# Cross-attention with split 16-bit products: result copies before the exp, context maxima two tiles earlier, a shorter context scale, the first low part transposed later

## The reference

```python
q = (x @ Wq + bq); k = (ctx @ Wk + bk); v = (ctx @ Wv + bv)     # 16 heads of 64
attn = softmax(q k^T / 8)                                         # per head, over 1444 keys
out  = (attn v) @ Wo + bo
z    = x + out
y    = (z - mean(z)) / sqrt(var(z) + 1e-5) * gamma + beta
```

## Time and profile before

| | |
|---|---|
| median of the runs | 945.15 us |
| the profiled execution, its own time | 943.91 us |
| its span in the profile | 942.0 us |
| busy PE / DVE / ACT / POOL | 892.3 / 830.2 / 754.6 / 281.9 us |
| granted PE clock, mean over the span | 0.989 of 2.4 GHz |

### The profile page before, as it was taken

How to read it: one execution, slowest core, us unless ns; L and a number is a source line. 1 busy time by engine, 2 the same in 40 slices (tenths; PEclk the granted TensorE clock), 3 DMA queues, 4 the chain that set the end, 5 groups by cost and what they waited for, 6 DMA issues and landing times.

```text
span 942.0 us, 25453 instructions
## 1 busy us (share of the span) xinstructions
PE 892.3 (95%) x10366; PEld 673.4 (71%) x10366; DVE 830.2 (88%) x1072; ACT 754.6 (80%) x1082; POOL 281.9 (30%) x368
## 2 busy tenths in 40 slices
PE   7797998999999999999999999999999999999996
PEld 6475876777777776777777777777777676677775
DVE  4897889999898999989799998989999798998983
ACT  3675978888888888888888878888888888888983
POOL 3051394413214141232404223141412424042001
PEclk9998999999999999999999999999999999999999
DMA  8676999999999999999999999999999999999995
GB/s 224 133 159 143 186 175 163 204 203 187 220 181 205 201 214 205 201 213 183 208 198 206 211 178 211 193 215 201 197 212 192 198 196 196 198 183 203 204 178 112
DMA packets 683065, 181.17 MB, mean 192 GB/s; under 512 B 654596, under 2 KB 682052, under 8 KB 682948
## 3 DMA queue, kind: packets, MB, share of 16 engines
q1 hardware_dynamic: 681332, 178.48, 99.3%
q10 hardware_dynamic: 1344, 0.53, 0.2%
q0 software_dynamic: 272, 0.53, 0.2%
HBM read 15.35 MB, written 0.82 MB: 17 GB/s over the span
## 4 chain that ended last, share of the span: by engine, by line
PE 51%; DVE 22%; issue 8%; DMA 8%; POOL 5%; ACT 4%; SPq 1%; POOLq 0%; DVEq 0%; ACTq 0%
PE ps L530 21%; PE ps L544 15%; DVE p_lo L765 9%; PE ps L549 8%; DVE nmax L750 8%; DMA pt_lo<-p_lo 7%; PE ps L399 4%; PE ps L393 2%; DVE c_max L670 1%; ACT p L868 1%; POOL c_lo L975 1%; POOL early_sb L1003 1%; ACT c_hi L850 1%; POOL c_scaled L1001 1%; ACT o_t L891 1%
## 5 line engine op out<-in xcount | busy, mean ns | idle before, releaser
L765 DVE SCALAR_TENSOR_TENSOR p_lo<-p,rinv,p_hi 128x1444 f16<-128x1444 f32 x200 | 352.3, 1762 | 19.5 <-DMA pt_lo<-p_lo 17.2
L868 ACT ACTIVATE p<-ps,nmax 128x1446 f32<-128x1446 f32 x200 | 292.2, 1461 | 89.8 <-DVE nmax L750 89.1
L750 DVE TENSOR_REDUCE nmax<-ps 128x1 f32<-128x1446 f32 x200 | 331.5, 1658 | 36.3 <-PE ps L530 32.6
L876 ACT ACTIVATE p_hi<-p,rinv 128x1444 f16<-128x1444 f32 x200 | 299.8, 1499 | 39.0 <-DVE rinv L758 37.5
L544 PE MATMUL ps<-pt_hi,c_hi 128*128 128x128 f16 (+1 forms) x2288 | 270.0, 217 | 27.9 <-ACT o_t L891 25.2
L544 PEld LDWEIGHTS ps<-pt_hi,c_hi 128*128 128x128 f16 x2288 | 216.0, 98 | 76.2 <-ACT o_t L891 64.1
L544 PE MATMUL ps<-pt_hi,c_lo 128*128 128x128 f16 (+1 forms) x2288 | 269.3, 217 | 0.0
L544 PEld LDWEIGHTS ps<-pt_hi,c_lo 128*128 128x128 f16 x2288 | 217.5, 98 | 12.0 <-issue 0.2
L530 PE MATMUL ps<-ct_hi,g_hi 128*128 128x482 f16 (+3 forms) x624 | 157.2, 370 | 2.1 <-DMA ct_hi<-c_hi 2.1
L549 PE MATMUL ps<-pt_lo,c_hi 128*128 128x128 f16 (+1 forms) x2288 | 157.5, 217 | 0.0
L530 PE MATMUL ps<-ct_hi,g_lo 128*128 128x482 f16 (+3 forms) x624 | 157.1, 370 | 0.0
(11 more groups left out here) (108 smaller groups left out, 654.0 us busy)
## 6 DMA issues: line engine op xcount, KB each, us to landing
c_raw<-in_ctx_dram SPq DMA_DIRECT2D x32, 256.0 KB
pt_hi<-p_hi SPq DMA_TRANSPOSE x200, 3.5
pt_lo<-p_lo SPq DMA_TRANSPOSE x200, 3.7
c_raw<-in_ctx_dram SPq DMA_DIRECT2D x16, 192.0 KB
c_raw<-in_ctx_dram SPq DMA_DIRECT2D x48, 18.0 KB
out_dram<-y SPq DMA_DIRECT2D x16, 50.0 KB
x_sb<-in_x_dram SPq DMA_DIRECT2D x1, 600.0 KB
o_t<-in_L_xattn_Wq_dram SPq DMA_DIRECT2D x2, 256.0 KB, 4.4
```

Source lines behind the costliest of these rows:

```text
L750: dve.tensor_reduce(nmax[:, n % RING:n % RING + 1], ps[:, bank:bank + 3, 0:KEYW], AX.XY, ALU.max, negate=True).then_inc(s_nm, 1)
L765: dve.scalar_tensor_tensor(out=p_lo[:, par, 0:KL], in0=p32[:, n % P32S, 0:KL], scalar=rinv[:, i:i + 1], in1=p_hi[:, par, 0:KL], op0=ALU.mu ...
L868: act.activation(p32[:, n % P32S, :].rearrange("p (k w) -> p k w", w=KEYW), ps[:, bank:bank + 3, 0:KEYW], ACT.Exp, bias=nmax[:, i:i + 1], ...
L876: act.activation(p_hi[:, par, 0:KL], p32[:, n % P32S, 0:KL], ACT.Copy, scale=rinv[:, i:i + 1]).then_inc(s_hi, 1)
```

## The change

- ACT: `take_result(n-4)` stands before `exponentials(n)` instead of behind it, in every tile.
- The thirds of the context's high part are at r = 4, 6, 7 instead of 4, 5, 6.
- The context maxima are at r = 6, 7, 8 instead of 8, 9, 10; the spreading matmul and `context_scale` at r = 10 instead of 11, except in window 0.
- `context_scale` is two DVE instructions instead of three: a constant column of 1e-30 joins the maxima, and the identity by which the matmul spreads them is scaled by 1/32 beforehand (`ident_part`), so that the reduction writes `unscale` directly.
- The subtraction and scaling of the layer norm (`norm_rows`) go from DVE to POOL, into `scale_rows`; z, zn, zg and y live in the space of `wo_sb`, now called `late_sb`.
- SP: `ct_hi` at r = 7, `ct_lo` at r = 8, and in window 0 at r = 9.

```diff
-    CMAX_AT = 8
+    CMAX_AT = 6
-    CT_LO_AT = 7
+    CT_LO_AT = 8
+    CT_LO_AT_FIRST = 9
...
-                dve.tensor_reduce(c_top[:, :], bank[:, 0:P], AX.X, ALU.max).then_inc(s_ctop, 1)
-                dve.wait_ge(s_ctop, b + 1)
...
-                dve.tensor_scalar(un, c_top[:, :], C_LEAST, 1.0 / C_RANGE, ALU.max, ALU.mult).then_inc(s_us, 1)
+                dve.tensor_reduce(un, bank[:, 0:P], AX.X, ALU.max).then_inc(s_us, 1)
...
-                if r == TOP_AT and w > 0:
-                    norm_rows(w - 1)
...
             for n in range(N + LAG):
+                if n >= LAG:
+                    take_result(n - LAG)
                 if n < N:
                     exponentials(n)
-                if n >= LAG:
-                    take_result(n - LAG)
...
+            pool.tensor_scalar(ident_part[:, :], ident[:, :], 1.0 / C_RANGE, 1.0, ALU.mult, ALU.mult).then_inc(s_part_id, 1)
...
             def scale_rows(b):
                 par = b % 2
+                pool.wait_ge(s_rd, b + 1)
+                pool.tensor_scalar(zn[:, par, :], z[:, par, :], mv[:, par, 0:1], rstd[:, par:par + 1], ALU.subtract,
+                                   ALU.mult).then_inc(s_zn, 1)
```

More of the change, by code:

```diff
@@ L58, in cross_attention_kernel @@
     STORE_AT = 2
-    CHI_AT = 4
+    CHI_AT = (4, 6, 7)
     FIN_AT = 6
-    CMAX_AT = 8
-    CT_HI_AT = 6
-    CT_LO_AT = 7
+    CMAX_AT = 6
+    CT_HI_AT = 7
+    CT_LO_AT = 8
+    CT_LO_AT_FIRST = 9
     ROWS_AT = 9
-    TOP_AT = 11
+    TOP_AT = 10
+    TOP_AT_FIRST = 11
     def first_tile(b):
@@ L111, in cross_attention_kernel @@
         ident = sb("ident", [P, P])
+        ident_part = sb("ident_part", [P, P])
         early_sb = sb("early_sb", [P, 4, PAIRS, P])
@@ L118, in cross_attention_kernel @@
             "p (b i q) -> p b i q", i=2, q=QL)
-        wo_sb = sb("wo_sb", [P, PAIRS, P])
+        late_sb = sb("late_sb", [P, PAIRS, P])
+        wo_sb = late_sb
+        z, zn, zg, y = [late_sb[0:QL, 2 * i:2 * i + 2, :] for i in range(4)]
         bv_sb = sb("bv_sb", [P, PAIRS])
@@ L177, in cross_attention_kernel @@
         s_axt = sem("ax_max_spread")
-        s_ctop = sem("context_max_on_every_partition")
+        s_part_id = sem("identity_over_range_ready")
         s_const = sem("constants_set")
@@ L193, in cross_attention_kernel @@
         s_axz = sem("ax_parts_zeroed")
+        s_cleast = sem("least_context_max_set")
         s_ax = sem("ax_group_max")
@@ L358, in _ @@
                     transpose_context_hi(w + 1)
-                if r == CT_LO_AT and w + 1 < B:
+                if r == (CT_LO_AT if w else CT_LO_AT_FIRST) and w + 1 < B:
                     transpose_context_lo(w + 1)
@@ L450, in spread_context_max @@
                 pe.wait_ge(s_cm, b + 1)
-                pe.matmul(bank[:, 0:P], spread(c_max[:, NT:NT + 1]), ident[:, :], start=True, stop=True).then_inc(s_top, 1)
+                pe.wait_ge(s_part_id, 1)
+                pe.matmul(bank[:, 0:P], spread(c_max[:, NT + 1:NT + 2]), ident_part[:, :], start=True, stop=True).then_inc(s_top, 1)
             def spread_ax_max(bank):
@@ L477, in _ @@
                     emptied(pe, J_A + 3)
-                    pe.wait_ge(s_ctop, 1)
+                    pe.wait_ge(s_us, 1)
                 project_queries(take(J_G + g), 0, g).then_inc(s_fill, 1)
@@ L566, in job @@
                     else:
-                        pe.wait_ge(s_ctop, b + 1)
+                        pe.wait_ge(s_us, b + 1)
                     if b < 3:
@@ L588, in job @@
                         mm.then_inc(s_fin, 1)
-                if r == TOP_AT and w + 2 < B:
+                if r == (TOP_AT if w else TOP_AT_FIRST) and w + 2 < B:
                     if w > 0:
@@ L660, in _ @@
             dve.memset(mhalf[:, :], -0.5)
+            dve.memset(c_max[:, NT:NT + 1], C_LEAST).then_inc(s_cleast, 1)
             dve.memset(p_lo[:, :, KL + 2 * KTAIL:KT * P], 0.0)
@@ L903, in _ @@
                 w, r = window(n)
-                if CHI_AT <= r < CHI_AT + NT and w + 1 < B:
-                    context_hi(w + 1, r - CHI_AT)
+                if r in CHI_AT and w + 1 < B:
+                    context_hi(w + 1, CHI_AT.index(r))
                 for k in ONCE.get(n, ()):
```

17 lines of the change are left out of this document (4 added, 13 removed).

## The result

The changed kernel takes 910.93 us (median of four runs, 907.61 to 912.4) against 944.12 us for the kernel before (four runs, 942.49 to 946.78): a ratio of 0.9641, 95% interval 0.9604 to 0.9678. The forecast was 914.5 us. The profiled execution took 911.81 us with a span of 909.9 us, so it is compared with the 942.0 us span of before.

The account below looks back on a forecast made before the run. PE's own work was taken to bound the kernel, with 5.3 us of waits per steady pair. 943.91 - 23.4 - 7.5 + 0.4 = 913.4 us, 914.5 as median; own range 907 to 920, taken overall 903 to 931.

Parts of the forecast that it names:

- PE's floor: Steady pairs: PE's own work needs 105.5 us of the 110.8, so 5.3 us per pair go to waits.
- Steady pairs: Six middle pairs of batches: each loses 1.4 us to waits instead of 5.3, together 23.4 us less.
- the end's share: Bare tiles near a window's end, held by DVE: about 1.2 of a window's 2.65 us lost, removed by moving the maxima.
- Copy first: ACT, every tile: exp 0.46 us later where ACT waited for nmax, at N + 2.16 (N = nmax start), hidden by 1.2 us of room.
- slower rival: ACT: the exp waits for `weigh` in each tile, 0.31 us per tile; about 971 us, chance 0.07.
- First pair: Windows 0 and 1: 7.5 us less, from -5.5 in window 0 and -2 in window 1.
- Last pair, drain and start: Both ends of the kernel: later exp costs 0.6 us at the end, 0.2 gained at the start; +0.4.
- Norm step to POOL: Layer norm on POOL: instruction of some 0.46 us; blocking DVE's low part costs 0 to 7 us, taken as 0.
- First low part: Window 0's 11.67 us tile falls to about 4.9 with the later `ct_lo`; gain 6.8 us.
- the stall stays: Tiles 4 to 6: transposed low parts set the time, 14 windows keep 1.3 us more; about 923 us, chance 0.24.
- The DMA rate: DMA transposes in steady pairs: 205 GB/s at 106 us per pair would still fit under the skill's 261 GB/s.

Follow-up runs that it names:

- k: Changed kernel with the context's first low part in window 0 transposed at r = 7 again instead of r = 9; 913.57 us.
- b: Kernel before with only the result copy moved ahead of the exp; 926.17 us.
- j: Changed kernel with maxima back at r = 8 to 10 and the spreading matmul and scale at r = 11; 916.69 us.
- a: Changed kernel with the result copy behind the exp again; 923.88 us.
- g: Changed kernel with 56 extra 128x128 copies on ACT, in out-projection tiles r = 6 to 9 of windows 2 to 15; 910.64 us.
- c: Kernel before with only the context's first low part in window 0 transposed at r = 9 instead of 7; 936.25 us.
- e: Changed kernel with the layer norm's subtraction and scaling back on DVE, ahead of the context scale; 913.99 us.
- l: Changed kernel with window 1's bias addition to x in four pieces and the norm step on DVE for all batches but the first; 905.79 us.
- i: Changed kernel with only the spreading matmul and scale at r = 11 again, maxima staying at r = 6 to 8; 909.85 us.
- h: Changed kernel with POOL's one bias addition to x in window 1 cut into four pieces of four batches; 905.19 us.

## Why the prediction was right

Point by point, by its own terms.

- **PE's floor, 105.5 us per pair.** Held: the shortest steady pair is 106.1 by the starts of the scores, with 3.74, 4.28 and 4.65 us in the three kinds of tile. Two small terms were missing: the tile behind the spreading matmul is 0.28 longer, not 0.2, and the tiles beside a pair's middle are 0.1 longer.
- **Steady pairs, -23.4.** Measured -23.5 on PE. That they agree to 0.1 us is luck: k, with the same instructions there, has -26.8. The copy does most of it (-18 alone, +13 if undone), the places +6 if undone: the parts overlap and do not add. Where a window loses its 2.65 us was read rightly (29.8 us in twelve windows, 2.5 each, 1.1 of it at the window's end, forecast 1.2). Which part of the change would take the end's share away was half wrong. I gave it to the maxima's new places, because "DVE holds PE in tiles in which PE has no heavy job". The runs show that with the copy first DVE's load, maxima and all, no longer holds PE (b and j: 3.74 us in tiles 10 and 12). What the maxima's places do is another thing, which the prediction does not have: they end PE's wait at the spreading matmul (4.2 us in b, 7.5 in j).
- **Copy first costs 0.46 us per exp, hidden by 1.2 us of room.** Half held. The exp that was to come at N + 2.16 comes at N + 2.02 in tiles r = 0, 1, 7 and 12, but at N + 1.69 as before in the query tiles r = 2 to 4 (539.83 - 538.14 in the rows above) and in tiles 9 to 11. In these DVE is late enough for `weigh` to have ended, the prediction's own "against" to its slower rival, which is out, with a query tile of 4.28 on PE and 4.12 on DVE. A bare tile's nmax starts lie 3.86 apart, forecast 3.88. The lag and the room were both sized too small: nmax trails PE's scores by 3.0 to 3.7 us at the medians of the steady tiles, where a has 2.0 to 2.2, so DVE runs 1.0 to 1.7 us further behind and not 0.3 to 0.6, and PE still keeps its pace; g's copies did not show either.
- **First pair, -7.5.** Measured -7.9 on PE, -7.3 by nmax, by two errors that cancel. By nmax window 0 went from 66.86 to 60.19 us, -6.7 against -5.5: the long tile lost 6.5, tiles 6 to 8 became 1.4 us longer by the maxima, as forecast, but 9, 11 and 12 together 1.4 shorter, which I had not counted. Of that 0.6 is tile 9, which a maximum left; tiles 11 and 12 are shorter in c too, where the maxima stay, so that there the end of the stall is enough. Window 1 went from 64.73 to 64.14, -0.6 against -2 (-1.5 on PE). The tile of the earlier trace rows did not change (8.24 us, now 8.25): room between engines does not help a stall on DVE in which `rinv`, and so `p_hi`, stands behind the blocked instruction on the same queue. That term was wrong in kind.
- **Last pair, drain and start, +0.4.** Measured on PE -0.2, -0.5 and 0. The slower ACT cycle is there (nmax starts 3.86 apart where before had 3.74 to 3.87), but DVE and ACT fell behind PE by it without PE having to wait: the 0.6 us were counted on the wrong engine.
- **Norm step to POOL, 0 of 0 to 7.** 0 in the steady windows (e, l). But the step takes 0.80 us on POOL at the median, not 0.46, and 2.32 in window 1 beside the low part; the instruction behind it takes 1.50 where before it took 0.46. No large wait ends on them; 0.5 us at the end does (e, l).
- **First low part, -6.8.** -7.1 in c's window 0, +7.0 in k's. In the medians -8 and -2.6 with wide scatter, of which the clock below explains a part at most.

Of the rivals, "the stall stays" (923 us) was the one to fear: the waits for transposes at r = 6 do remain, but PE lost 3.2 us at r = 6 and 7 in twelve windows, not 1.3 in each. The DMA rate that went with it was mis-sized: the bytes of a steady pair in 106 us make 201 x 110.8 / 106 = 210 GB/s, not 205; 208 were measured.

## What to carry to other kernels

A short copy that frees an accumulator belongs ahead of a long instruction on the same in-order queue, if the queue has a gap per tile somewhere else: here a copy of 0.35 us, moved out of a free gap, took 13 to 18 us off the time. A value that PE needs is better finished two tiles before the matmul than one: here waits of up to 1.1 us in front of it, 7.5 us in twelve windows, stayed in the time, while 56 extra copies on ACT, which trails PE, did not show. A stall inside one engine's own queue (the blocked low part) was not absorbed by slack between engines here; splitting the instruction that blocked it shortened the tile by 2 us.

## What was unexpected of the hardware

**The clock in window 0.** The long tile of the earlier trace rows was not only a wait. Stretches of 6 us of the kernel before, then of after, then of i (the same instructions as after in window 0), with the columns of the earlier trace rows:

```profile
72.00:78.00 6.00, 1.91 (x34) 1.73 (x32) 2.65 (x3) 1.45 (x2) 1.18 (x3) 1.00 0.79 167
78.00:84.00 6.00, 5.12 (x16) 2.92 (x17) 4.25 (x8) 4.28 (x7) 0.00 (x0) 0.58 0.95 215
```

```profile
72.00:78.00 6.00, 3.97 (x45) 3.07 (x42) 5.74 (x9) 5.16 (x9) 2.64 (x3) 1.00 0.70 158
78.00:84.00 6.00, 6.00 (x74) 4.49 (x73) 5.56 (x13) 4.36 (x6) 0.28 (x1) 1.00 0.94 175
```

```profile
72.00:78.00 6.00, 3.97 (x43) 3.57 (x41) 5.68 (x8) 5.16 (x9) 2.85 (x3) 0.82 0.67 151
78.00:84.00 6.00, 6.00 (x44) 3.75 (x44) 3.70 (x5) 1.73 (x2) 0.00 (x0) 0.61 0.56 126
```

In before PE worked 1.91 of 6 us while it waited for `ct_lo`, and the granted clock then was 0.58 on average, which is 1.2 GHz for most of the stretch: part of the 11.67 us is PE at half speed after the wait. In the changed kernel PE works 3.97 of those 6 us, and the clock stayed at 1.00 in one execution. In i, with the same instructions and the same 3.97 us, it fell already in the first stretch (0.82) and was 0.61 in the second, and the tile is 7.63 us long instead of 5.13. So window 0 can come out either way, and this is one source of 2.5 us of difference between executions. It does not explain all of the scatter: the four runs of after took 907.61 to 912.4 us with mean clocks of 0.992 and 0.993.

In the executions profiled, the blocked low part has such a price too. From 136 to 142 us, behind the tile of 8.25 us, the granted clock of after is 0.72; in h, where PE works 5.69 us from 130 to 136 instead of 4.21, it is 1.00.

**A blocked instruction.** The low part reads two inputs from SBUF and began 0.31 us after a POOL instruction of 4.52 us; it ended 1.54 us after that one did, where alone it takes 1.72. In smaller overlaps POOL's side stretches as well: POOL's scaling of 400 columns took 0.60 us alone and 1.81 to 2.02 beside the low part. The Trainium skill (SBUF — State Buffer, Who interferes with whom) says that such a pair shares a read interface and that the second to issue is blocked until the first is done; the 5.75 us and experiment h agree.

**DMA.** The steady pairs now move 206 to 212 GB/s, 208 over all six, where before had 201: the same bytes in less time. ACT's waits for the transposes of `p_lo` fell from 32.2 to 15.3 us. So a reported busy share of 1.05, as before had, was no limit yet; after has 1.12.
